# Writing the result in groups of four chunks, with the per-pixel factors spread by four 32-row matmuls

## Chip, core and metric

The kernel runs on one core of a Trainium2 chip. The metric is the device time of one execution in microseconds (us); lower is better. The engines are named as in the profile: PE is TensorE (matmuls and transposes; PEld is its loading of weights), DVE is VectorE, ACT is ScalarE, POOL is GpSimd, SP is SyncE, which only issues DMAs here.

## What is computed

The input `x` is 8 images of 128 x 128 pixels with 32 channels in fp32. Four layers are added to it one after the other, each on a group-normalised `x`. The change touches only the last layer and the writing of the result:

```python
x = x + _L0_conv_ref(_gn(x), ...)     # per-channel GELU mixer
x = x + _L1_conv_ref(_gn(x), kernel)  # 4 x 4 FIR filter
x = x + _L2_conv_ref(_gn(x), ...)     # windowed channel attention
x = x + _L3_conv_ref(_gn(x), W1, b1, gamma, beta)

def _L3_conv_ref(inputs, W1, b1, gamma, beta):
    kernel = centers @ W1 + b1                  # 9 weights for each inner pixel
    weighted = patches * kernel                 # the 3 x 3 patch around it
    yout = zeros.at[...].add(weighted)          # scattered back by addition
    yn = (yout - mean) * rsqrt(var + 1e-3) * gamma + beta   # mean, var over all pixels and images
    return where(yn >= 0, yn, 0.3 * yn)
```

Since each weight multiplies the pixel at which its product lands, `yout` at a pixel is the normalised input there times one number s, the sum of up to nine weights. So the last layer is v = (x - mean) * s, then statistics of v over everything, then a scale, a bias, the leaky step max(y, 0.3 y), and the sum with x.

## The kernel before, in words

`X` holds all pixels in SBUF: partition 32g + c is channel c of image g in a set of four images (a "sample", s = 0 or 1), and the free axis runs over the 16384 pixels of an image, column w by column w, 128 rows h each. Work goes by *chunks* of 512 columns of `X`; a sample has 32 chunks. Here a chunk n is made of the four image columns w = n, 32 + n, 64 + n, 96 + n (`columns(s, n)`).

Each sample passes stages 0 to 7, and every engine waits at each stage's end for the others (`stage_end`). Stages 0 to 4 load, transpose and run the first three layers, stage 5 computes the weights, stage 6 sums them to s and stores it transposed in `ST` (128 partitions for 32 chunks x 4 images, 512 columns). Two later places use s:

- **Stage 7** measures v. For each chunk `spread_s` (line 256) is one fp32 matmul that copies the four rows of `ST` of that chunk to all 128 partitions of a PSUM bank: the weights are a 128 x 128 0/1 matrix out of `sel`. Four banks are used in turn. For even chunks DVE makes v from PSUM (line 897); for odd ones ACT copies (lines 662, 663) and POOL multiplies (line 1038). DVE takes the statistics of all (`bn_stats`, line 889), in a loop of four chunks.
- **The output stage** comes once, after both samples and after the small steps for the overall statistics. For each chunk, in this order: `spread_s` (PE), `scaled` = v (DVE, line 939), `norm` (ACT, line 668), `leaky` (DVE, line 944), the sum with `X` (POOL, line 1054), four transposes to pixel-major order (PE, line 525), `lay` into the output buffer (ACT, line 677), and, for every four chunks, four DMAs of 256 KB (SP, line 304). `row`, a ring of eight 512-column buffers, holds a chunk from `scaled` to the transposes. Each engine does its steps in the order of its own program: DVE does `scaled(n + 2)` and then `leaky(n)`, ACT `norm(n + 4)` and then `lay(n)`, PE `out_s(n + 5)` and then `out_t(n)`. Engines wait for one another by counting semaphores alone (`s_fv`, `s_fy`, `s_fl`, `s_fo`, `s_ft`, `s_fe`). The stage does the first sample's 32 chunks and then the second's.

Of the kernel before, what the change touches and what calls it, by code (L numbers as in the profile page):

```python
# [22 lines left out]
P = 128  # L23
B, H, W, C = 8, 128, 128, 32
G = P // C
# [19 lines left out]
K9 = 9  # L45
# [4 lines left out]
ROWS = 8  # L50
# [16 lines left out]
def build(nc, x, consts, choose, out):  # L67
# [5 lines left out]
    with ctx:  # L73
# [40 lines left out]

        def rows4(v):
            return v.rearrange("p (b h) -> p b h", b=4)
# [33 lines left out]
        sel, _e = part(_e, [W // 4, P])  # L150
        vb, _v = part(_e, [DEEP, BANK])
        xd, _ = part(_v, [RING, BANK])
        U, _ = part(_v, [3, W, G])

        row, _o = part(0, [ROWS, BANK])
        assert _o <= (W + 2) * G * K9 and LOADS * G * LW * C <= (W + 2) * G * K9 + DEEP * BANK
        ob, _ = part(_e, [RING, G, 4, 4, C])
# [70 lines left out]
        s_fv = rsem("out_v_ready", "dve", DEEP)  # L228
        s_fy = sem("out_y_ready")
        s_fl = sem("out_l_ready")  # L230
        s_fo = sem("out_sum_ready")
        s_ft = rsem("out_transposed", "pe", ROWS)
        s_fe = rsem("out_chunk_ready", "act", DEEP)
        s_out = [sem(f"chunk_stored{u}") for u in range(RING)]
# [33 lines left out]
        def _(sp):  # L268
# [10 lines left out]
            for s in range(NS):  # L279
# [6 lines left out]
                for k in range(STAGES):  # L286
                    if k == 5:
                        sp.dma_start(sel[:, :, :], choose[:, :, :]).then_inc(s_sel, 16)
# [7 lines left out]
            with sp.Fori(0, NS) as s:  # L296
                with sp.Fori(0, 4) as i:
                    for u in range(RING):

                        sp.wait_ge(s_fe, after(s * NB + i * 8 + (4 * u + 3), DEEP))  # L300
                        for g in range(G):
                            o = out.rearrange("i h (b w) c -> h i b (w c)", b=4)
                            o = o[:, ds(s * G + g, 1), :, ds(i * (8 * C) + 4 * C * u, 4 * C)]
                            sp.dma_start(o.rearrange("h a b w -> h (a b) w"),
                                         ob[:, u, g, :, :, :].rearrange("p b w c -> p b (w c)")).then_inc(s_out[u], 16)
            for u in range(RING):
                sp.wait_ge(s_out[u], NS * 4 * 64 + 64)
# [3 lines left out]
        def _(pe):  # L311
# [4 lines left out]
            with pe.Fori(0, NS) as s:  # L316
# [185 lines left out]
                pe.wait_ge(s_sel, s * 16 + 16)  # L502
                for n in range(NB):
# [9 lines left out]
            with pe.Fori(0, NS) as s:  # L513
# [15 lines left out]
                for n in range(DEEP + 1):  # L529
                    out_s(n)  # L530
# [599 lines left out]
```

## Time and profile before

| | |
|---|---|
| median of 3 executions | 1149.85 us (1148.54 to 1150.21) |
| span of the profiled execution, first to last instruction | 1148.0 us |
| mean granted TensorE clock of that execution | 0.923 of full speed |
| stage 7 of the second sample | about 954 to 992 us of the span |
| output stage, first spreading matmul to last ACT copy | 997.1 to 1142.0 us |
| last copy to the end of the span (the last four DMAs) | 5.98 us |

The profiled execution's own time is not listed apart from the three above; what lies around its span is taken as the median less the span, 1.85 us. The profile page gives the busy time of each engine, the chain of waits that ended last, and groups of instructions; the trace behind it gives every instruction in order of time, with the idle time of its engine before it and the instruction that ended this idle time in square brackets. Matmul records of fp32 come in pairs (two passes for one matmul).

### The profile page before, as it was taken

The page shows a single profiled execution, that of the slowest core. Times are in us where ns is not written, and L with a number is a line of the kernel's source. Part 1 is how long each engine was busy: PE and PEld are TensorE (multiplying, and loading weights), DVE is VectorE, ACT ScalarE, POOL GpSimd, SP SyncE. Part 2 cuts the span into 40 slices and gives each one's busy share as a digit, 9 for nine tenths or more (in the row PEclk, how much of TensorE's full clock was granted, in tenths as well). Part 3 has the DMA queues.
Part 4 walks back from the last instruction along what each step waited for, and adds up shares of the span by engine and source line. Part 5 has one row for each costly group of instructions (what it writes and reads, how often), then busy time and mean ns, then how long its engine had stood idle before and what let it go on. Part 6 is the DMA issues. An engine that isn't in the chain of part 4 may idle for free. (4 is left out here: it accounts for less than half of the span.)

```text
span 1148.0 us, 22784 instructions
## 1 busy us (share of the span) xinstructions
PE 952.7 (83%) x6876; PEld 650.8 (57%) x6876; DVE 867.1 (76%) x1211; ACT 693.3 (60%) x860; POOL 317.6 (28%) x265
## 2 busy tenths in 40 slices
PE   5699977979989977845999949799999788676774
PEld 4333327968878875334433349688778683233332
DVE  7477788877757944876687878877769646799796
ACT  5799972323358853547999923234388563366564
POOL 0000009400026720510000066000077403466565
PEclk9799998989989988987999979989999898899897
DMA  9100000000000010233000000000000200024334
GB/s 294 37 0 0 0 0 1 0 1 1 0 1 1 0 73 5 69 114 107 0 0 0 0 1 1 1 1 0 1 1 0 74 0 1 0 86 135 106 114 146
DMA packets 51301, 39.32 MB, mean 34 GB/s; under 512 B 1600, under 2 KB 50880, under 8 KB 51008
## 3 DMA queue, kind: packets, MB, share of 16 engines
q1 hardware_dynamic: 51264, 38.85, 10.7%
q8 instruction: 20, 0.33, 0.1%
q14 instruction: 17, 0.14, 0.0%
HBM read 22.07 MB, written 16.78 MB: 34 GB/s over the span
## 5 line engine op out<-in xcount | busy, mean ns | idle before, releaser
L337 PE MATMUL ps<-work,cst 128*128 128x512 f32 x512 | 237.0, 610 | 17.5 <-ACT work L557 13.7
L337 PEld LDWEIGHTS ps<-work,cst 128*128 128x128 f32 x512 | 94.5, 193 | 158.8 <-issue 144.4
L256 PE MATMUL ps<-ST,work 128*128 x256 | 131.1, 635 | 9.7 <-DVE work L897 7.1
L557 ACT ACTIVATE work<-X,l0s 128x2048 f32 x64 | 136.6, 2140 | 2.6 <-SPq L294 2.6
L564 ACT ACTIVATE work<-ps 128x2048 f32<-128x2048 f32 x64 | 123.1, 1923 | 8.2 <-PE ps L337 8.0
L1019 POOL TENSOR_TENSOR work<-cst,ksum 128x512 f32<-128x512 f32 x64 | 66.2, 1055 | 203.2 <-SPq L294 174.4
L806 DVE TENSOR_TENSOR work<-ps,cst 64x512 f32<-64x512 f32 x128 | 88.2, 689 | 39.1 <-PE ps L404 37.3
L984 POOL TENSOR_TENSOR co<-mv,cst 128x1 f32<-128x1 f32 x8 | 1.5, 191 | 392.1 <-DVEq L246 302.4
L450 PE MATMUL ps<-work,cst 128*64 128x128 f32 x1024 | 103.6, 287 | 6.7 <-ACT work L621 6.7
L586 ACT ACTIVATE work<-ps 128x512 f32<-128x512 f32 x80 | 47.8, 598 | 100.5 <-PE ps L357 100.5
L450 PEld LDWEIGHTS ps<-work,cst 128*64 128x64 f32 x1024 | 88.4, 141 | 18.7 <-issue 9.9
L1054 POOL TENSOR_TENSOR work<-X,work 128x512 f32<-128x512 f32 x64 | 82.3, 1288 | 59.6 <-DVE work L944 59.6
L368 PE MATMUL ps<-cst,work 128*128 128x143 f32 x640 | 96.6, 295 | 2.6 <-DVE X L756 2.2
L726 DVE SCALAR_TENSOR_TENSOR work<-work,cst 128x2048 f32<-128x2048 f32 x32 | 75.2, 2351 | 24.3 <-ACT work L564 24.1
L944 DVE SCALAR_TENSOR_TENSOR work<-work 128x512 f32<-128x512 f32 x64 | 92.2, 1445 | 0.0
L595 ACT ACTIVATE work<-ps 128x512 f32<-128x512 f32 x64 | 38.2, 597 | 86.7 <-PE ps L404 86.7
L368 PEld LDWEIGHTS ps<-cst,work 128*128 128x128 f32 x640 | 85.8, 195 | 7.0 <-DVE X L756 5.9
L668 ACT ACTIVATE work<-work,bns 128x512 f32<-128x512 f32 x64 | 52.1, 814 | 59.9 <-DVE work L939 59.9
L621 ACT ACTIVATE work<-work 32x512 f32 (+1 forms) x128 | 80.4, 628 | 5.9 <-SPq L294 3.9
L525 PEld LDWEIGHTS ps<-cst,work 128*128 128x128 f32 x256 | 29.2, 150 | 87.1 <-POOL work L1054 87.1
L525 PE MATMUL ps<-cst,work 128*128 128x128 f32 x256 | 45.6, 305 | 39.1 <-POOL work L1054 38.9
L256 PEld LDWEIGHTS ps<-ST,work 128*128 128x128 f32 x256 | 46.6, 204 | 54.2 <-issue 30.5
(99 smaller groups left out, 1774.3 us busy)
## 6 DMA issues: line engine op xcount, KB each, us to landing
work<-x SPq DMA_DIRECT2D x32, 512.0 KB, 4.9
out<-work SPq DMA_DIRECT2D x64, 256.0 KB, 2.8
work<-choose SPq DMA_DIRECT2D x2, 2048.0 KB, 8.4
cst<-consts SPq DMA_DIRECT2D x1, 1009.5 KB, 9.6
cst<-consts SPq DMA_DIRECT2D x1, 64.0 KB, 2.0
```

What stands on the lines that cost most here:

```text
L256: return nc.tensor.matmul(ps[:, bank, :], sel[:, n, :], ST[:, ds(s * (4 * H), 4 * H)], start=True, stop=True)
L337: last = pe.matmul(ps[:, 4 * (m % 2) + b, :], wg[:, m, :], yb[:, m, b * BANK:(b + 1) * BANK], start=True, stop=True)
L368: last = pe.matmul(ps[:, DEEP + 2 * (q % 2) + par, at:at + OW * OH], patch[:, q, k, :], c("fir"), start=True, stop=True)
L450: last = pe.matmul(o[:, :, :, hd * CK:hd * CK + CK], wq[:, hd, :], mvg, start=(hd == 0), stop=(hd == HEADS - 1))
L525: last = pe.transpose(ps[:, DEEP + n % DEEP, w * P:w * P + P], row[:, n % ROWS, w * H:w * H + H], ident)
L557: act.activation(yb[:, m, :], X[:, ds(s * PIX + i * CHUNK, CHUNK)], ACT.Gelu, scale=l0s[:, m:m + 1], bias=l0s[:, MULTI + m:MULTI + m + 1]) ...
L564: act.activation(zb[:, m % 2, :], ps[:, 4 * (m % 2):4 * (m % 2) + 4, :].rearrange("p a b -> p (a b)"), ACT.Gelu).then_inc(s_zs, 1)
L621: last = act.activation(mh[C * g:C * g + C, u, :, g, :], src, ACT.Copy)
L726: dve.scalar_tensor_tensor(acc if m < MULTI - 1 else x_in, zb[:, m % 2, :], c("w2")[:, m:m + 1], acc if m else x_in, ALU.mult, ALU.add).th ...
L806: last = dve.tensor_tensor(o, k_in, bias, ALU.add)
L944: dve.scalar_tensor_tensor(row[:, u, :], row[:, u, :], LEAKY, row[:, u, :], ALU.mult, ALU.max).then_inc(s_fl, 1)
L1054: pool.tensor_tensor(rows4(row[:, u, :]), columns(s, n), rows4(row[:, u, :]), ALU.add).then_inc(s_fo, 1)
```

## The change

The output stage handles *groups* of four chunks (`TILES = 4`), 16 groups in all (`NS * GROUPS`), running through both samples without a break.

- `spread_group` replaces `spread_s`: four matmuls of 32 rows each. The rows of `ST` are stored in another order (four small copies in stage 6 instead of one), so that the rows of the four chunks of a group lie in four different 32-row parts; each matmul takes one part and writes one PSUM bank. `sel` shrinks from 32 matrices to 8 and is loaded by four DMAs.
- Stage 7 uses all eight banks, four to a group; DVE's loop covers eight chunks instead of four.
- In the output stage `scaled` is still done chunk by chunk (four in a row), `norm` and `leaky` are one operation of 2048 columns for a group, the sum is two of 1024 columns, the transposes and `lay` go in two halves. DVE does `scaled(q)` and then `leaky(q - 1)`; ACT `norm(q)` and then `lay(q - 3)`; PE the spreading of q and then the transposes of q - 3. `row` holds four groups, the output buffer three.
- PE's loop over samples is written out.

```diff
+TILES = 4
+GROUPS = W // 4 // TILES
+OUT_ROWS, OUT_RING = 4, 3
...
-        def spread_s(s, n, bank):
-
-            return nc.tensor.matmul(ps[:, bank, :], sel[:, n, :], ST[:, ds(s * (4 * H), 4 * H)], start=True, stop=True)
+        def spread_group(s, j, bank):
+
+            for r in range(TILES):
+                rows = slice(C * r, C * r + C)
+                last = nc.tensor.matmul(ps[:, bank + r, :], sel[rows, j, :], ST[rows, s * (4 * H):(s + 1) * (4 * H)],
+                                        start=True, stop=True)
+            return last
...
-                for n in range(NB):
-                    pe.wait_ge(s_so if n % 2 else s_v[0], slot(s * (NB // 2) + n // 2))
-                    spread_s(s, n, n % DEEP).then_inc(s_sc, 1)
+                for j in range(GROUPS):
+                    if j >= 2:
+                        pe.wait_ge(s_v[0], after(s * (NB // 2) + 2 * j - 3))
+                        pe.wait_ge(s_so, after(s * (NB // 2) + 2 * j - 3))
+                    spread_group(s, j, j % 2 * TILES).then_inc(s_sc, 1)
...
-                for n in range(DEEP + 1):
-                    out_s(n)
-                for n in range(NB):
-                    if n + DEEP + 1 < NB:
-                        out_s(n + DEEP + 1)
-                    out_t(n)
+            for q in range(NS * GROUPS):
+                if q:
+                    pe.wait_ge(s_fv, TILES * q)
+                spread_group(q // GROUPS, q % GROUPS, 0).then_inc(s_fc, 1)
+                if q >= 3:
+                    out_transposed(q - 3)
...
+            def norm(q):
+                act.wait_ge(s_fv, TILES * q + TILES)
+                s = q // GROUPS
+                y = row[:, q % OUT_ROWS, :, :].rearrange("p b n -> p (b n)")
+                act.activation(y, y, ACT.Identity, scale=bns[:, 12 + s:13 + s], bias=bns[:, 15:16]
+                               ).then_inc(s_fy, 1)
...
-                dve.tensor_copy(s_rows[:, :], ps[:, 7, :]).then_inc(s_ss, 1)
+                for r in range(TILES):
+                    by_tile = s_rows[:, :].rearrange("p (b r j g) -> p b r j g", b=4, r=TILES, g=G)[:, :, r, :, :]
+                    src = ps[:, 7, :].rearrange("p (b j r g) -> p b r j g", b=4, r=TILES, g=G)[:, :, r, :, :]
+                    last = dve.tensor_copy(by_tile, src)
+                last.then_inc(s_ss, 1)
...
+            def scaled(q):
+                s, j = divmod(q, GROUPS)
+                dve.wait_ge(s_fc, q + 1)
+                if q >= OUT_ROWS:
+                    dve.wait_ge(s_ft, 2 * (q - OUT_ROWS) + 2)
+                for r in range(TILES):
+                    dve.scalar_tensor_tensor(row[:, q % OUT_ROWS, :, r * H:r * H + H], columns(s, TILES * j + r),
+                                             vall[:, 4 * s + 3:4 * s + 4], rows4(ps[:, r, :]), ALU.add, ALU.mult
+                                             ).then_inc(s_fv, 1)
+
+            def leaky(q):
+                dve.wait_ge(s_fy, q + 1)
+                y = row[:, q % OUT_ROWS, :, :].rearrange("p b n -> p (b n)")
+                dve.scalar_tensor_tensor(y, y, LEAKY, y, ALU.mult, ALU.max).then_inc(s_fl, 1)
+
+            for q in range(NS * GROUPS):
+                scaled(q)
+                if q:
+                    leaky(q - 1)
+            leaky(NS * GROUPS - 1)
...
-                        pool.tensor_tensor(rows4(row[:, u, :]), columns(s, n), rows4(row[:, u, :]), ALU.add
-                                           ).then_inc(s_fo, 1)
+            for q in range(NS * GROUPS):
+                s, j = divmod(q, GROUPS)
+                pool.wait_ge(s_fl, q + 1)
+                for b in range(0, 4, 2):
+                    y = row[:, q % OUT_ROWS, b:b + 2, :]
+                    pool.tensor_tensor(y, group_columns(s, j, b), y, ALU.add).then_inc(s_fo, 1)
```

How the program of DVE reads in the middle of the output stage, with the semaphores each row waits for (line 939 is `scaled`, line 944 `leaky`), before:

```order
L939 ISA [waits out_transposed,out_s_spread]
L939 SCALAR_TENSOR_TENSOR work<-X,vall,ps 128x512
L944 SCALAR_TENSOR_TENSOR work<-work 128x512 [waits out_y_ready]
L937 REGISTER_ALU
L939 ISA [waits out_transposed,out_s_spread]
```

and in the changed kernel (line 954 is `scaled`, line 961 `leaky`):

```order
L954 SCALAR_TENSOR_TENSOR work<-X,vall,ps 128x4x128 [waits out_transposed,out_s_spread]
L954 SCALAR_TENSOR_TENSOR work<-X,vall,ps 128x4x128 x3
L961 SCALAR_TENSOR_TENSOR work<-work 128x2048 [waits out_y_ready]
L954 SCALAR_TENSOR_TENSOR work<-X,vall,ps 128x4x128 [waits out_transposed,out_s_spread]
L954 SCALAR_TENSOR_TENSOR work<-X,vall,ps 128x4x128 x3
```

One `leaky` of 2048 columns now stands behind four `scaled`, and the four share one wait for PE.

PE's program at the same place (line 256 is the spreading matmul, line 525 the transposes), before:

```order
L256 MATMUL ps<-ST,work 128x512 [waits out_v_ready]
L525 MATMUL ps<-cst,work 128x128 [waits out_chunk_ready,out_sum_ready]
L525 MATMUL ps<-cst,work 128x128 x3
L516 REGISTER_ALU
L256 MATMUL ps<-ST,work 128x512 [waits out_v_ready]
```

and in the changed kernel (line 265 is the spreading matmul, line 532 the transposes; `out_half_laid` is `s_fe`, `out_half_sum_ready` is `s_fo`):

```order
L265 MATMUL ps<-ST,work 128x512 [waits out_v_ready]
L265 MATMUL ps<-ST,work 128x512 x3
L532 MATMUL ps<-cst,work 128x128 [waits out_half_laid,out_half_sum_ready]
L532 MATMUL ps<-cst,work 128x128 x7
L532 MATMUL ps<-cst,work 128x128 [waits out_half_laid,out_half_sum_ready]
L532 MATMUL ps<-cst,work 128x128 x7
```

The spreading of a group is now four matmuls in a row, in front of 16 transposes that wait twice.

DVE's loop in stage 7, before (line 897 makes v of an even chunk, line 889 measures), one turn of four chunks from its second half to the branch and the first row of the next:

```order
L897 ISA [waits s_spread]
L897 SCALAR_TENSOR_TENSOR work<-X,co,ps 128x512
L889 ISA [waits odd_v_ready]
L889 BN_STATS stats<-work 128x6
L887 REGISTER_ALU
L889 ISA [waits even_v_ready]
L889 BN_STATS stats<-work 128x6
L889 ISA [waits odd_v_ready]
L889 BN_STATS stats<-work 128x6
L885 REGISTER_ALU
L885 COMPARE_AND_BRANCH
```

and in the changed kernel at the same point of the turn (lines 910 and 902), where the next group's first chunk now comes in between:

```order
L902 ISA [waits even_v_ready]
L902 BN_STATS stats<-work 128x6
L909 REGISTER_ALU
L910 ISA [waits s_spread]
L910 SCALAR_TENSOR_TENSOR work<-X,co,ps 128x512
L902 ISA [waits odd_v_ready]
L902 BN_STATS stats<-work 128x6
```

The measuring of a group's last chunk moved behind the making of v for the next group's first one, at every second group.

## Rows read from the trace of the kernel before

**Rows 1.** The page: busy time of each engine, share, count.

```profile
PE 952.7 (83%) x6876; PEld 650.8 (57%) x6876; DVE 867.1 (76%) x1211; ACT 693.3 (60%) x860; POOL 317.6 (28%) x265
```

**Rows 2.** Windows: from:to, length, busy PE, PEld, DVE, ACT, POOL, clock, DMA.

```profile
955.00:992.00 37.00, 29.93 (x64) 11.61 (x62) 31.02 (x48) 19.29 (x32) 20.36 (x16) 0.96 0.00 0
1004.00:1064.00 60.00, 42.27 (x170) 19.48 (x168) 60.00 (x59) 37.13 (x57) 36.78 (x30) 0.99 0.35 106
```

**Rows 3.** Timeline, one period of the output stage: start, duration, instruction, idle before.

```profile
1040.90 0.73 DVE L939 SCALAR_TENSOR_TENSOR work<-X,vall,ps 128x512 f32<-128x512 f32 x1
1041.23 1.27 POOL L1054 TENSOR_TENSOR work<-X,work 128x512 f32<-128x512 f32 x1 [0.80 <-DVE work L944]
1041.56 1.49 DVE L944 SCALAR_TENSOR_TENSOR work<-work 128x512 f32<-128x512 f32 x1
...
1043.30 1.27 POOL L1054 TENSOR_TENSOR work<-X,work 128x512 f32<-128x512 f32 x1 [0.80 <-DVE work L944]
```

**Rows 4.** Line L944 by itself: duration in ns, least, median, most.

```profile
L944 DVE SCALAR_TENSOR_TENSOR work<-work x64: 678/1484/1747, 1003.0 to 1136.1; 128x512 f32<-128x512 f32 x64
```

**Rows 5.** Groups of instructions by shape: busy us, mean ns, idle before.

```profile
L726 DVE SCALAR_TENSOR_TENSOR work<-work,cst 128x2048 f32<-128x2048 f32 x32 | 75.2, 2351 | 24.3 <-ACT work L564 24.1
L965 POOL TENSOR_TENSOR cst<-cst 128x128 f32<-128x128 f32 x1 | 0.5, 459 | 11.9 <-DMA cst<-consts 11.9
L557 ACT ACTIVATE work<-X,l0s 128x2048 f32 x64 | 136.6, 2140 | 2.6 <-SPq L294 2.6
L564 ACT ACTIVATE work<-ps 128x2048 f32<-128x2048 f32 x64 | 123.1, 1923 | 8.2 <-PE ps L337 8.0
L677 ACT ACTIVATE work<-ps 128x512 f32<-128x512 f32 x64 | 37.1, 580 | 8.2 <-PE ps L525 8.2
L883 DVE COPY ST<-ps 128x512 f32 x2 | 1.4, 692 | 2.2 <-PE ps L498 2.2
```

**Rows 6.** Timeline, TensorE in stage 3: matmuls on the whole array, then column-tiled ones.

```profile
791.15 1.06 PE L404 MATMUL ps<-cst,work 128*128 128x128 f32 x8
792.14 1.08 PE L414 MATMUL ps<-work 128*32 128x128 f32 x32
```

**Rows 7.** Timeline, the start of the output stage.

```profile
997.08 7.26 PE L256 MATMUL ps<-ST,work 128*128 x11
...
999.22 0.75 DVE L939 SCALAR_TENSOR_TENSOR work<-X,vall,ps 128x512 f32<-128x512 f32 x1
...
1000.88 0.75 DVE L939 SCALAR_TENSOR_TENSOR work<-X,vall,ps 128x512 f32<-128x512 f32 x1 [0.90 <-PE ps L256]
...
1003.99 1.27 POOL L1054 TENSOR_TENSOR work<-X,work 128x512 f32<-128x512 f32 x1 [5.68 <-DVE work L944]
```

**Rows 8.** Timeline, between the first sample's last chunk and the second's first.

```profile
1071.26 0.75 DVE L939 SCALAR_TENSOR_TENSOR work<-X,vall,ps 128x512 f32<-128x512 f32 x1 [5.26 <-PE ps L256]
```

**Rows 9.** Timeline, the end of the output stage.

```profile
1134.12 3.75 DVE L944 SCALAR_TENSOR_TENSOR work<-work 128x512 f32<-128x512 f32 x3
...
1135.85 4.37 POOL L1054 TENSOR_TENSOR work<-X,work 128x512 f32<-128x512 f32 x3 [0.80 <-DVE work L944]
...
1139.05 2.34 PE L525 MATMUL ps<-cst,work 128*128 128x128 f32 x8 [0.56 <-POOL work L1054]
...
1141.42 0.60 ACT L677 ACTIVATE work<-ps 128x512 f32<-128x512 f32 x1 [0.62 <-PE ps L525]
```

**Rows 10.** Timeline, stage 7 of the second sample.

```profile
956.25 0.75 DVE L897 SCALAR_TENSOR_TENSOR work<-X,co,ps 128x512 f32<-128x512 f32 x1 [2.79 <-PE ps L256]
...
958.01 0.72 ACT L662 ACTIVATE work<-X,co 128x512 f32 x1 [18.52 <-PE ps L256]
...
963.18 0.75 DVE L897 SCALAR_TENSOR_TENSOR work<-X,co,ps 128x512 f32<-128x512 f32 x1
...
963.99 3.70 PE L256 MATMUL ps<-ST,work 128*128 x8 [1.26 <-DVE work L897]
...
990.55 1.87 DVE L889 BATCH_NORM_STATS2 stats<-work 128x512 f32 x3
```

More of the change, by code:

```diff
@@ L149, in build @@
         s_rows, _e = part(_e, [W * G])
-        sel, _e = part(_e, [W // 4, P])
         vb, _v = part(_e, [DEEP, BANK])
-        xd, _ = part(_v, [RING, BANK])
+        xd, _e7 = part(_v, [RING, BANK])
         U, _ = part(_v, [3, W, G])
-        row, _o = part(0, [ROWS, BANK])
-        assert _o <= (W + 2) * G * K9 and LOADS * G * LW * C <= (W + 2) * G * K9 + DEEP * BANK
-        ob, _ = part(_e, [RING, G, 4, 4, C])
+        row, _o = part(0, [OUT_ROWS, 4, BANK])
+        ob, _o = part(_o, [OUT_RING, G, 4 * TILES, C])
+        sel, _s = part(MW + 7168 - 8 * P, [W // 4 // TILES, P])
+        assert max(_e7, _o) <= MW + 7168 - 8 * P
+        assert LOADS * G * LW * C <= (W + 2) * G * K9 + DEEP * BANK
         ring_sems = {}
@@ L295, in _ @@
                     sp.wait_ge(s_stage, s * (STAGES * ENG) + (k + 1) * ENG)
[L296 to L307, printed above, removed]
+            for q in range(NS * GROUPS):
+                s, j = divmod(q, GROUPS)
+                sp.wait_ge(s_fe, 2 * q + 2)
+                for g in range(G):
+                    o = out[s * G + g, :, :, :].rearrange("h (b w) c -> h b (w c)", b=4)
+                    sp.dma_start(o[:, :, TILES * C * j:TILES * C * (j + 1)],
+                                 ob[:, q % OUT_RING, g, :, :].rearrange("p (b w) c -> p b (w c)", b=4)
+                                 ).then_inc(s_out[q % OUT_RING], 16)
+            for u in range(OUT_RING):
+                sp.wait_ge(s_out[u], len(range(u, NS * GROUPS, OUT_RING)) * G * 16)
         @block.tensor
@@ L315, in _ @@
             pe.wait_ge(s_ident, 16)
-            with pe.Fori(0, NS) as s:
+            for s in range(NS):
                 with pe.Fori(0, W // LW // LOADS) as i:
@@ L654, in _ @@
                 stage_end(act, s, 6)
[L656 to L659 removed]
+                with act.Fori(0, GROUPS // 2) as i:
+                    for v in range(1, 2 * TILES, 2):
+                        u = v % TILES
+                        nn = s * (NB // 2) + i * TILES + v // 2
+                        act.wait_ge(s_sc, s * GROUPS + i * 2 + (v // TILES + 1))
@@ new lines, in norm, with lay @@
+            def norm(q):
[4 more added lines that the diff above has]
+                               ).then_inc(s_fy, 1)
+            def lay(q):
+                for hf in range(2):
+                    act.wait_ge(s_ft, 2 * q + hf + 1)
+                    if hf == 0 and q >= OUT_RING:
+                        act.wait_ge(s_out[q % OUT_RING], q // OUT_RING * G * 16)
+                    half = slice(2 * TILES * hf, 2 * TILES * hf + 2 * TILES)
+                    o = ob[:, q % OUT_RING, :, half, :].rearrange("p g m c -> p m g c")
+                    src = ps[:, TILES + 2 * hf:TILES + 2 * hf + 2, :].rearrange("p b (n g c) -> p (b n) g c", n=TILES, g=G)
+                    act.activation(o, src, ACT.Copy).then_inc(s_fe, 1)
@@ L693, in _ @@
+            for q in range(NS * GROUPS):
+                norm(q)
+                if q >= 3:
+                    lay(q - 3)
+            lay(NS * GROUPS - 3)
+            lay(NS * GROUPS - 2)
+            lay(NS * GROUPS - 1)
         @block.vector
```

133 lines of the change are left out of this document (44 added, 89 removed).

## The prediction

> **What bounds the kernel now.** The page's busy times [rows 1] name no one engine, and the stages have different limits, so I read the two touched stages by themselves. In the windows [rows 2] the reader should see that DVE is busy for all 60.00 us of the output stage's 60, while POOL shows 36.8, ACT 37.1 and PE 42.3, with TensorE's clock granted at 0.99 of full. But a busy DVE is not a working one. `leaky` takes 0.68 us at its quickest and 1.48 at its median [rows 4]. The timeline of one period [rows 3] shows why. POOL's sum starts at 1041.23 and ends at 1042.50. `leaky` starts at 1041.56, inside it, and ends at 1043.05, which is 0.55 behind POOL's end: DVE's two-input operation from SBUF has stood still until POOL was done. `scaled`, which has PSUM as an input, starts at 1040.90, is overlapped by POOL too, and still takes its 0.73. POOL's next sum starts 0.25 after `leaky`'s end (1043.30). So the period of 2.07 us is POOL 1.27, plus what remains of `leaky` 0.55, plus 0.25 for the semaphore: a closed loop of two engines that take turns at SBUF. It is 8.27 us for four chunks.
>
> Around the loop there are three fixed losses. At the start, PE's clock is at 1.2 GHz and the first spreading matmuls come 1.66 us apart (999.22 and 1000.88 [rows 7]). Between the samples DVE waits 5.26 us for PE [rows 8], because PE does the second sample's spreading only after the first's last transposes. At the end the pipeline runs out [rows 9] and the last ACT copy ends at 1142.02.
>
> In stage 7 [rows 10], DVE goes at 4.18 us for four chunks ((990.55 + 1.87 - 963.18) / 7 turns) and is busy 31.0 us of 37 [rows 2]: it is close to its own limit except at the start.
>
> **The output stage, by a ledger of SBUF turns.** What may not overlap is POOL's sums and DVE's `leaky`.
>
> - *POOL, 1024 columns.* 128 columns with the same kind of inputs take 0.46 [rows 5], 512 take 1.27 [rows 3], so 2.11 ns a column, and 1024 columns 1.27 + 1.08 = 2.35 us. Bounds: 2.16 if nothing is fixed in it (2.11 ns x 1024), 2.54 if all is proportional (2 x 1.27). 32 of them: 75.2 us (69 to 81).
> - *`leaky`, 2048 columns.* The same kind of operation takes 2.35 us alone [rows 5]; behind a POOL operation the 512-column one needed 0.55 instead of 0.68, so 2.22. 16 of them: 35.5 us (34 to 38).
> - *Hand-over.* Before, POOL idled 0.25 of every period. Now POOL has two operations for each `leaky`, and four `scaled` (0.66 apart by [rows 3], 2.71 together) lie between two `leaky`. `leaky(q)` arrives about 2.6 us after `leaky(q-1)` ended, just when POOL's first half ends (0.25 + 2.35). If DVE gets in between the halves, POOL never runs dry; if it has to wait for both, 0.25 comes back for each group, 4 us in all. In the tail, where POOL had three sums to do and DVE was waiting, the 3 `leaky` were finished within 3.75 us while the 3 sums took 4.37 [rows 9], so DVE did get in between. I take 1 us (0 to 4).
>
> Sum: 111.7 us (103 to 123), 7.0 a group against 8.27.
>
> *When it starts.* PE can start the first group at 997.1 as before [rows 7]. At the low clock one matmul is 1.66; how long do four with 32 rows take? No row shows row-tiled ones. Stage 3 has column-tiled ones: 8 records on the whole array take 1.06, 32 records on quarter arrays 1.08 [rows 6], so four run side by side. If rows do the same, a group takes about what one chunk took, say 2.5 us at the low clock and 1.3 at the full one (0.92 a matmul by 3.70 for four [rows 10], plus start-up). The bound from the other side is one after the other: 3.7 to 3.9, or 6.6 to 7.0 at the low clock. I take side by side, as the nearest row. Then `scaled(0)` is 999.6 to 1002.3, the second group's spreading waits for it (one set of four banks) until 1004.8, `scaled(1)` ends at 1007.5, and only then comes `leaky(0)`; `norm(0)` (2.14 [rows 5]) is hidden behind this. So the first turn begins at 1007.5. Before, POOL's first sum started at 1003.99: the larger groups cost some 6 us of filling.
>
> The Trainium skill (TensorEngine Tiling (Array Packing), Performance Considerations and Tiling Modes) says that tiles of 32 rows run up to 4 times faster, and TensorE: Matmul & The Clock Gate (Part 3) gives 3.07 times as measured. By that figure a group would take 4 x 0.92 / 3.07 = 1.2 us at the full clock and 2.2 at the low one, an estimate that leaves the sum where it is. The tiling page also says that a change of tiling mode drains TensorE. That speaks against a change that switches twice a group, but by the busy times below PE has some 3 us to spare in each group.
>
> *Who else could be late.* For a group: DVE 2.64 + 2.22 = 4.9; ACT `norm` 2.14 and two `lay` of 1.03 each (0.58 and the slope of [rows 5], (1923 - 580) / 1536 ns a column), 4.2; PE 1.3 + 4 x 0.65 = 3.9 at the full clock, 2.5 + 4 x 1.12 = 7.0 at the low one (8 transposes took 2.34 there [rows 9]). All are below or at 7.0. A group's spreading has from the end of `scaled(q-1)` to that of `leaky(q-2)`, about 4.3 us. So these are hidden; if the clock stays low, PE just about becomes a second limit. The break between samples is gone, since the groups run through.
>
> *The end.* The turns end at 1007.5 + 111.7 = 1119.2. Then the last half's 8 transposes at the low clock, 2.3, and `lay` 1.1: 1122.6. Before it was 1142.02 [rows 9]. **-19.4 us.** The last four DMAs are as before (1 MB after the last copy, 5.98 us). In the steady part 1 MB has to leave every 7.0 us instead of 8.3; DMA was busy 0.35 of the time [rows 2], so that stays hidden.
>
> **Stage 7.** At its start PE runs at the low clock, ACT's first odd chunk waits until 958.01 for the second matmul, and DVE's second group begins at 963.18 [rows 10]. With four banks filled at once, and the other four without any wait behind them, ACT can start with DVE at about 956.5, the second odd chunk follows directly, and the second group comes 2 to 3 us earlier. After that the steady turn gains little: DVE's six operations are 3.8 us of 4.18, and the loop now ends every eight chunks instead of four. I take -2.5 for each sample, **-5.0 us** (0 to -8). A group's spreading is asked for when the group two before is read, a whole turn ahead (4 us), and takes 1.3.
>
> **Stage 6.** Four copies of 128 columns replace one of 512, 692 ns [rows 5], so each needs at least a quarter of that, 0.17, and at most all of it. The slope of the two POOL sizes above leaves about a seventh of an operation as fixed; three more fixed parts of 0.1 make +0.3 a sample: **+0.6 us** for both (0 to 4). It is on the path, PE waits for it. The loads of `sel`, the written-out loop of PE: nothing, since they lie in stages where SP and PE's program are not what is waited for; in the output stage PE waited for data, not for its program.
>
> **Sum.** -19.4 - 5.0 + 0.6 = -23.8 us. Against the profiled execution (1148.0 and 1.85 around it, which is the median 1149.85): **1126 us**.
>
> **The rivals.**
>
> - *Less is saved in turns (0.14).* POOL's cost is proportional and hand-overs come back: 81.3 + 37.6 + 4 = 123 us, end at 1134 instead of 1122.6, and stage 7 gives 2: 1140 us. For it: I have only two sizes of POOL operation.
> - *The 32-row matmuls run one after the other at the full clock (0.08).* For it: no row shows them. In the output stage 3.9 fits in the 4.3 us window, but the first two groups are late by about 5; in stage 7 PE needs 3.9 of 4.18, starts cold with 7.0 for each of two groups, and costs about 7.5 a sample over the forecast: 1126 + 5 + 15 = 1146 us.
> - *They run one after the other and the clock is at the low level: slower (0.05).* Place: PE's own order, spreading of q and 16 transposes. Price: 7.0 + 4.5 = 11.5 us a group in the output stage against 8.6 before ((1142.0 - 1004.0) / 16), and 7.0 against 4.2 in stage 7: +46 +45, 1240 us. It decides from the point where PE's work for a group passes 8.6 us. Against it: where PE was busy 70 to 80% its clock was 0.96 to 0.99 [rows 2], and serial matmuls would keep it busier than that.
> - *Long operations do not exclude each other (0.07).* If only the short operations stood in each other's way, DVE's 4.9 us would be the period: 2.1 x 15 less, 1094 us. The Trainium skill (SBUF — State Buffer, Who interferes with whom) says that the pair of SBUF ports shared by DVE and POOL is an exclusive lock, held for the whole instruction by whichever starts first; by that rule the ledger holds for any length and this rival falls.
>
> The forecast has 0.66. **Range:** 1115 (turns at 2.16 and 2.1, stage 7 at -8) to 1140 (the first rival), which holds the forecast and that rival, 0.80. About 0.2% is what a measurement of this kernel can tell from no change. Faster by more: 0.66 + 0.14 + 0.08 + 0.07 = 0.95, less 0.02 for a chance that the late ones end at no change: 0.93; same 0.02; slower 0.05.
>
> **What would show it.** In the profile after: 2048-column `leaky` records of up to 4.6 us that end some 2.2 us after a POOL sum; POOL sums of 2.35; about 7.0 us from one group's first sum to the next; POOL busy nearly 70% of the output stage; the four spreading matmuls starting together; `leaky(0)` beginning at about 1002.5 us of the span (1007.5 less the 5 of stage 7); no wait of 5 us in the middle. Wrong if the spreading of a group takes over 4.3 us, if POOL's sums are over 2.5, or if DVE waits for `norm` or for PE in every group.

## The result, and the profile after

The changed kernel takes 1124.12 us (median of 4, 1124.04 to 1124.86) against 1150.03 us for the kernel before in the same series (median of 4): a ratio of 0.9775, with a 95% interval of 0.9761 to 0.9789, 25.9 us less. 1126 was forecast. The profiled execution took 1124.1 us with a span of 1122.0.

By place: the output stage's first spreading matmul starts at 993.38 instead of 997.08 us of the span, so everything ahead of it gave 3.7 us. From there to the last ACT copy it is 122.8 us instead of 144.9, which gave 22.1. The last DMAs gave 0.2. (Not all of the 3.7 us lies in stages 6 and 7; see "Why the prediction was right".)

The timeline of one group in the changed kernel (start, duration, engine, line, operation, what it waited for), which answers to [rows 3]:

```profile
1053.69 2.71 DVE L954 SCALAR_TENSOR_TENSOR work<-X,vall,ps 128x512 f32<-128x512 f32 x4
1053.85 4.65 POOL L1065 TENSOR_TENSOR work<-X,work 128x1024 f32<-128x1024 f32 x2 [2.23 <-DVE work L961]
1056.32 4.33 DVE L961 SCALAR_TENSOR_TENSOR work<-work 128x2048 f32<-128x2048 f32 x1
1056.43 2.09 ACT L680 ACTIVATE work<-work,bns 128x2048 f32<-128x2048 f32 x1 [2.99 <-DVE work L954]
1056.45 0.31 PEld L265 LDWEIGHTS ps<-ST,work 32*128 32x128 f32 x8 [2.04 <-DVE work L954]
1056.45 1.83 PE L265 MATMUL ps<-ST,work 32*128 32x512 f32 x8 [1.80 <-DVE work L954]
1058.43 1.92 ACT L691 ACTIVATE work<-ps 128x1024 f32<-128x1024 f32 x2
1059.55 3.27 PEld L532 LDWEIGHTS ps<-cst,work 128*128 128x128 f32 x16 [2.79 <-issue]
1059.58 3.65 PE L532 MATMUL ps<-cst,work 128*128 128x128 f32 x16 [1.29 <-ACT work L691]
1060.57 2.71 DVE L954 SCALAR_TENSOR_TENSOR work<-X,vall,ps 128x512 f32<-128x512 f32 x4
1060.73 4.67 POOL L1065 TENSOR_TENSOR work<-X,work 128x1024 f32<-128x1024 f32 x2 [2.23 <-DVE work L961]
```

The reader should see the same two engines taking turns. POOL sums from 1053.85 to 1058.50, both halves without a gap. `leaky` starts at 1056.32 inside them, ends at 1060.65, 2.15 us behind POOL's end, and POOL starts again 0.08 later. The period is 6.88 us for four chunks where it was 8.27. It matters which half `leaky` meets. A narrower window (1057 to 1060) shows POOL's second half by itself:

```profile
1056.15 2.35 POOL L1065 TENSOR_TENSOR work<-X,work 128x1024 f32<-128x1024 f32 x1
```

`leaky` came 0.17 us after it had started, so it waited for this half alone, 2.18 us, and then needed 2.15. It is the same in all 13 groups of the steady part: `leaky` starts 0.15 to 0.18 us behind the second half's start. The lines of the two operations by themselves (ns least, median, most) say that the durations are the rule too:

```profile
L961 DVE SCALAR_TENSOR_TENSOR work<-work x16: 2278/4338/4352, 1003.2 to 1102.0; 128x2048 f32<-128x2048 f32 x16
L1065 POOL TENSOR_TENSOR work<-X,work x32: 2341/2355/4327, 1005.5 to 1111.0; 128x1024 f32<-128x1024 f32 x32
```

The start and the end of the stage (timeline), which answer to [rows 7] and [rows 9]:

```profile
993.38 2.09 PE L265 MATMUL ps<-ST,work 32*128 32x512 f32 x8
995.61 2.72 DVE L954 SCALAR_TENSOR_TENSOR work<-X,vall,ps 128x512 f32<-128x512 f32 x4 [0.21 <-PE ps L265]
998.39 2.09 PE L265 MATMUL ps<-ST,work 32*128 32x512 f32 x8 [2.92 <-DVE work L954]
1003.18 2.29 DVE L961 SCALAR_TENSOR_TENSOR work<-work 128x2048 f32<-128x2048 f32 x1
1005.55 4.68 POOL L1065 TENSOR_TENSOR work<-X,work 128x1024 f32<-128x1024 f32 x2 [11.00 <-DVE work L961]
...
1102.13 11.24 POOL L1065 TENSOR_TENSOR work<-X,work 128x1024 f32<-128x1024 f32 x4 [2.23 <-DVE work L961]
1115.20 1.02 ACT L691 ACTIVATE work<-ps 128x1024 f32<-128x1024 f32 x1 [1.05 <-PE ps L532]
```

The first `leaky` begins at 1003.18, the last sum ends at 1113.37, the last copy at 1116.22. Windows of stage 7 and of the output stage (from:to, length, busy PE, PEld, DVE, ACT, POOL, clock, DMA), for [rows 2]:

```profile
955.00:992.00 37.00, 12.18 (x50) 3.52 (x50) 30.68 (x51) 17.50 (x30) 20.37 (x19) 0.54 0.00 0
1012.00:1100.00 88.00, 55.19 (x298) 37.76 (x296) 88.00 (x66) 49.19 (x38) 60.70 (x26) 0.75 0.48 143
```

TensorE's clock is lower in both: 0.54 against 0.96, and 0.75 against 0.99.

### The profile page after: what moved, and what is told of

It is laid out like the page before. It is cut to its first block and busy times, and to the rows that moved or that the text cites. A ratio compares the mean times of both kernels' runs of the same rounds, so it can differ in the third digit from the quotient of the medians.

```text
span 1122.0 us, 21703 instructions
## 1 busy us (share of the span) xinstructions
PE 888.2 (79%) x6876; PEld 634.5 (57%) x6876; DVE 842.4 (75%) x1169; ACT 672.3 (60%) x780; POOL 311.0 (28%) x233
## 3 DMA queue, kind: packets, MB, share of 16 engines
q1 hardware_dynamic: 51360, 35.71, 10.4%
## 5 line engine op out<-in xcount | busy, mean ns | idle before, releaser
L265 PE MATMUL ps<-ST,work 32*128 32x512 f32 x256 | 57.7, 991 | 47.8 <-DVE work L954 18.6
L378 PEld LDWEIGHTS ps<-cst,work 128*128 128x128 f32 x640 | 86.2, 196 | 7.2 <-DVE X L765 4.8
L1065 POOL TENSOR_TENSOR work<-X,work 128x1024 f32<-128x1024 f32 x32 | 76.6, 2417 | 42.2 <-DVE work L961 42.2
L496 PE MATMUL ps<-cst,work 128*128 128x96 f32 x512 | 63.2, 291 | 14.9 <-ACT work L660 14.9
L1049 POOL TENSOR_TENSOR work<-work 128x512 f32<-128x512 f32 x32 | 40.4, 1266 | 124.0 <-ACT work L674 124.0
L367 PE MATMUL ps<-cst,work 128*128 128x128 f32 x320 | 51.0, 284 | 28.8 <-DVE work L788 28.8
L336 PE MATMUL ps<-cst,work 128*128 128x128 f32 x256 | 41.0, 325 | 40.8 <-DVE work L720 28.1
L496 PEld LDWEIGHTS ps<-cst,work 128*128 128x128 f32 x512 | 62.9, 207 | 15.3 <-ACT work L660 15.3
```

The lines of the kernel that those rows point to most:

```text
L265: last = nc.tensor.matmul(ps[:, bank + r, :], sel[rows, j, :], ST[rows, s * (4 * H):(s + 1) * (4 * H)], start=True, stop=True)
L378: last = pe.matmul(ps[:, DEEP + 2 * (q % 2) + par, at:at + OW * OH], patch[:, q, k, :], c("fir"), start=True, stop=True)
L496: last = pe.matmul(ps[:, u, w * COLS:w * COLS + COLS], xc[:, u, w * H:w * H + H], c("w9"), start=True, stop=True)
L1065: pool.tensor_tensor(y, group_columns(s, j, b), y, ALU.add).then_inc(s_fo, 1)
```

## The experiments

Each was timed beside the kernel before on the same chip. The changed kernel was not timed again with them; where a run is compared with its 1124.1 us, that rests on the kernel before, which came out at 1149.9 to 1150.5 us in every series.

**1. Waits with constants (`old_written_out`).** The kernel before; in its output stage every loop is a Python loop:

```diff
-            with pool.Fori(0, NS) as s:
-                with pool.Fori(0, NB // ROWS) as i:
+            for s in range(NS):
+                for i in range(NB // ROWS):
```

(the same for PE, ACT, DVE and SP)

> The kernel before, with the loops of the output stage written out on all five engines, so that waits have constants instead of registers; the same instructions in the same order otherwise. Theory A: of the 0.25 us between the end of DVE's leaky step and POOL's next sum, 0.12 to 0.17 were the register instruction ahead of the sum; the period falls from 2.07 to about 1.92 us and the time by 7 to 11 us (1139 to 1143). Rival B: the 0.25 us are the semaphore's own way, and the changed kernel's 0.08 comes from something in its grouping: within 2 us of 1150.

1139.2 us, ratio 0.9901 (0.9886 to 0.9916). A period of its timeline:

```profile
1039.94 1.26 POOL L1054 TENSOR_TENSOR work<-X,work 128x512 f32<-128x512 f32 x1 [0.63 <-DVE work L944]
1040.44 1.31 DVE L944 SCALAR_TENSOR_TENSOR work<-work 128x512 f32<-128x512 f32 x1
1041.83 1.27 POOL L1054 TENSOR_TENSOR work<-X,work 128x512 f32<-128x512 f32 x1 [0.63 <-DVE work L944]
```

POOL starts 0.08 us after `leaky`'s end (1041.75) instead of 0.25, and the period is 1.89 instead of 2.07. In the kernel before, POOL's program has a register instruction in front of each sum (line 1054 by itself, ns least, median, most); in this run there is none:

```profile
L1054 POOLq FUSED_REGOPS  x64: 121/121/150, 1003.7 to 1137.9; - x64
```

So of what I had called "the semaphore", 0.17 us were this instruction, 0.12 by its record, and what lies around it. 64 times 0.17 makes 10.9, and 10.7 us were measured. That is about two fifths of the change's gain, and it needs no grouping.

**2. No break between the samples (`old_continuous`).** The same, with all 64 chunks as one sequence on every engine:

```diff
-                for n in range(NB):
-                    if n + DEEP + 1 < NB:
-                        out_s(n + DEEP + 1)
-                    out_t(n)
+            for n in range(NS * NB):
+                if n + DEEP + 1 < NS * NB:
+                    out_s(n + DEEP + 1)
+                out_t(n)
```

> The kernel before with the output stage written out (1139.2 us) and, beyond that, all 64 chunks in one sequence, so that PE spreads the second sample's first chunks while the first sample's last ones are still under way. Theory A: the break between the samples, in which DVE waits 5.3 us and POOL starts 12.2 us behind the last sum of the first sample's steady part, goes; 4 to 7 us less than 1139.2, so 1132 to 1135. What the changed kernel has beyond this (1124.1) is then stages 6 and 7 (3.8) and the grouping proper (4 to 7). Rival B: the break was mostly a tail that now comes once in another place: 1137 to 1139.

1134.4 us (1131.5 to 1135.4), ratio 0.9865 (0.9839 to 0.9891): 4.8 less than experiment 1, within what was expected, though this one's runs spread more. In its trace the one interval of four chunks that took 13.0 us across the break takes 7.6 like the others.

**3. Stages 6 and 7 alone (`only_stage7`).** The changed kernel up to the output stage, then the old output stage, with one 32-row matmul for a chunk:

```diff
+        def spread_one(s, n, bank):
+
+            rows = slice(C * (n % TILES), C * (n % TILES) + C)
+            return nc.tensor.matmul(ps[:, bank, :], sel[rows, n // TILES, :], ST[rows, s * (4 * H):(s + 1) * (4 * H)],
+                                    start=True, stop=True)
```

> The changed kernel's stages 0 to 7 (groups of four in stage 7, four small copies in stage 6, PE's sample loop written out) with the output stage of the kernel before, in its loops, each chunk spread by one 32-row matmul. Theory A (the trace of the changed kernel): stages 6 and 7 give 3.8 us up to the start of the output stage, and nothing else changes: 1145 to 1148. Rival B: the order of DVE in stage 7 costs what the start gains: within 1 us of 1150. Rival C: the small matmuls lower TensorE's clock in the output stage (they do half the array's work in a chunk): PE gets late in places and the time goes above 1150.

1187.7 us, ratio 1.0331 (1.031 to 1.0352): much slower, in the direction of rival C and far beyond what I had thought of. Its windows in the output stage:

```profile
1010.00:1060.00 50.00, 50.00 (x99) 19.90 (x99) 22.58 (x34) 21.54 (x34) 20.80 (x18) 0.50 0.28 84
```

PE is busy for all 50 us and its clock stays at 1.2 GHz in this stretch. So:

**4. The same with 128 rows in the output stage (`only_stage7_128`).**

```diff
-            rows = slice(C * (n % TILES), C * (n % TILES) + C)
-            return nc.tensor.matmul(ps[:, bank, :], sel[rows, n // TILES, :], ST[rows, s * (4 * H):(s + 1) * (4 * H)],
+            return nc.tensor.matmul(ps[:, bank, :], sel[:, n, :], ST[:, s * (4 * H):(s + 1) * (4 * H)],
                                     start=True, stop=True)
```

> The kernel of the run with only stages 6 and 7 changed (1187.7 us), but in the output stage each chunk is spread by one matmul with all 128 rows again; stage 7 keeps its groups of 32-row matmuls, and everything else is the same (sel is 32 matrices wide for it). Theory A (the rows of the array that a matmul uses decide the clock): the granted clock of the output stage goes from 0.5 back to 0.99, the spreading matmul's two records from 2.07 to 1.02 us, the period from 3.0 to 2.07, and the time to 1145 to 1148. Rival B: the low clock comes from stage 7 or from waits between PE and DVE that feed on themselves: the clock stays low and the time above 1180.

1146.0 us, ratio 0.9968 (0.9958 to 0.9977). The same stretch of it:

```profile
1010.00:1060.00 50.00, 35.43 (x142) 16.00 (x140) 50.00 (x50) 31.10 (x48) 30.73 (x25) 1.00 0.42 126
```

Clock 1.00, PE busy 35.4 us. The two kernels differ only in the rows of that matmul and the table behind it, and by 42 us. This run also measures what all the rest of the change gives without the grouping of the output stage: 3.9 us by the medians. That is not stages 6 and 7 alone: in its trace the output stage starts 2.6 us earlier than before, and the interval of four chunks across the break between the samples is 1.1 us shorter (12.9 instead of 14.0); there too PE's loop over samples is written out.

**5. One after the other (`serial`).** In the changed kernel, each 32-row matmul waits for the one before:

```diff
+        s_one = sem("one_spread")
+        spreads = [0]
...
+                if r < TILES - 1:
+                    last.then_inc(s_one, 1)
+                    spreads[0] += 1
+                    nc.tensor.wait_ge(s_one, spreads[0])
```

> The changed kernel, but each of the four 32-row matmuls of a group waits on a semaphore until the one before it has ended, in stage 7 and in the output stage. Theory A (my rival priced at 1146 us): one after the other they take 4 us at the full clock and 7 at the low one; stage 7 asks for a group each 4.3 us and gets slow, the output stage has some 4 us of room; 12 to 25 us more than the changed kernel, most of it in stage 7. Rival B: TensorE has room for them everywhere: less than 3 us more. Rival C: the clock stays at the low level and the output stage's period goes to 10 or 11 us: over 60 us more.

1229.7 us, ratio 1.0692 (1.0676 to 1.0708), 105.6 over the changed kernel. Two rows of its timeline, the spreading of one group and what waits for it:

```profile
1134.39 8.45 PE L268 MATMUL ps<-ST,work 32*128 32x512 f32 x8
1130.89 2.72 DVE L961 SCALAR_TENSOR_TENSOR work<-X,vall,ps 128x512 f32<-128x512 f32 x4 [4.22 <-PE ps L268]
```

A group takes 8.45 us at the low clock, against 1.14 at the full clock and 2.09 at the low one side by side. The clock was 0.58 in the output stage although PE was busy 164 us of 180 (1040 to 1220). Rival C is what happened, and both stages pay: stage 7 takes 59.0 us a sample instead of 38.0, the output stage 185.2 instead of 122.8.

**6. Four sums of 512 columns (`pool_quarters`).**

```diff
-                for b in range(0, 4, 2):
-                    y = row[:, q % OUT_ROWS, b:b + 2, :]
-                    pool.tensor_tensor(y, group_columns(s, j, b), y, ALU.add).then_inc(s_fo, 1)
+                for b in range(4):
+                    y = row[:, q % OUT_ROWS, b:b + 1, :]
+                    last = pool.tensor_tensor(y, group_columns(s, j, b), y, ALU.add)
+                    if b % 2:
+                        last.then_inc(s_fo, 1)
```

(`group_columns` gives one column block instead of two)

> The changed kernel with POOL's sum as four operations of 512 columns for a group instead of two of 1024. Theory A (ledger of turns at SBUF): four take 5.0 to 5.1 us instead of 4.66, the period goes from 6.89 to about 7.3 us and the time up by 5 to 7 us (1129 to 1131). Rival B: not the ledger but the chain of latencies sets the period: within 1 us of 1124. Rival C: with more gaps between POOL's operations DVE gets in earlier, POOL never idles, and the period stays or falls below 6.9: 1118 to 1124.

1126.9 us, 2.7 over the changed kernel (ratio to the kernel before 0.9806, 0.9791 to 0.9821, against 0.9775). Windows of its output stage:

```profile
1012.00:1100.00 88.00, 59.32 (x302) 37.35 (x300) 71.70 (x67) 50.66 (x39) 88.00 (x50) 0.73 0.48 143
```

POOL is busy for all 88 us, and from one group's first sum to the next it takes 6.96 us in the mean of the trace. One group's `leaky` and the POOL sum behind it (timeline, 1070 to 1071):

```profile
1068.77 2.54 DVE L961 SCALAR_TENSOR_TENSOR work<-work 128x2048 f32<-128x2048 f32 x1
1069.12 3.31 POOL L1065 TENSOR_TENSOR work<-X,work 128x512 f32<-128x512 f32 x1
```

`leaky` arrives during one sum, waits for that one only (0.4 us here), and goes ahead of the next, whose record stretches from 1.27 to 3.31 us meanwhile. In every group with `leaky` between sums the trace shows this. So the hand-over is hidden (rival C's mechanism), and the longer sums cost slightly more than that saves (A's): 6.96 against 6.90. The time lies between A's range and C's. The period accounts for 0.9 of the 2.7 us; in the trace another 0.9 lies ahead of the output stage, in code that is the same.

**7. One sum of 2048 columns (`pool_whole`).**

```diff
-                for b in range(0, 4, 2):
-                    y = row[:, q % OUT_ROWS, b:b + 2, :]
-                    pool.tensor_tensor(y, group_columns(s, j, b), y, ALU.add).then_inc(s_fo, 1)
+                y = row[:, q % OUT_ROWS, :, :]
+                pool.tensor_tensor(y, group_columns(s, j, 0), y, ALU.add).then_inc(s_fo, 2)
```

(`group_columns` gives all four column blocks)

> The changed kernel with POOL's sum as one operation of 2048 columns for a group instead of two of 1024. Theory A (ledger): 2048 columns take about 4.5 us, the period goes from 6.89 to 6.7 to 6.8, and the end comes 2 us later since all transposes of the last group wait for the whole sum: 1121 to 1125. Rival B: the transposes and ACT's copies, which all start later, now set the period with TensorE's clock low: 1128 or more.

1125.0 us, ratio 0.9781 (0.9764 to 0.9797): not told apart from the changed kernel. A sum takes 4.53 us and the period is 6.82 where nothing else is late, but the transposes start later: the last copy ends 4.8 us behind the last sum instead of 2.85.

**8. Without the leaky step (`no_leaky`).**

```diff
-                               ).then_inc(s_fy, 1)
+                               ).then_inc(s_fl, 1)
...
             for q in range(NS * GROUPS):
                 scaled(q)
-                if q:
-                    leaky(q - 1)
-            leaky(NS * GROUPS - 1)
```

(the first two lines are ACT's `norm`, which now releases POOL)

> The changed kernel without the leaky step (negative values are not scaled by 0.3; the output is not the reference's): DVE has only the four products of a group, POOL sums what ACT normalised. Theory A (POOL and DVE's leaky take turns at SBUF): the period falls from 6.89 to POOL's own 4.7 us and the time by 25 to 33 us (1091 to 1099), POOL's sums keep their 2.35 us and never wait. Rival B: PE at the low clock (2.1 and 3.7 us a group) is next and holds the period near 5.8: 1105 to 1110. Rival C: the leaky step was not what POOL waited for: 1118 or more.

1092.3 us in one execution. Windows:

```profile
1010.00:1070.00 60.00, 42.00 (x312) 27.94 (x312) 35.76 (x53) 49.65 (x38) 59.47 (x26) 0.96 0.65 193
```

POOL is busy 59.5 of 60 us and the groups follow every 4.64 us. Nothing else needed the remaining 2.2 us of the period: they were `leaky`'s turn.

**9. DVE's order in stage 7 (`s7_order`).** The changed kernel, with the last chunk of a group measured before the next group's first product:

```diff
                     for v in range(2 * TILES):
+                        if v % TILES == 0 and v:
+                            measure_v(v - 1)
                         if v % 2 == 0:
...
-                        if v:
+                        if v % TILES:
                             measure_v(v - 1)
```

> The changed kernel, but in stage 7 DVE measures a group's last chunk before it makes v of the next group's first one, as before the change (still eight chunks to a loop). Theory A: the changed order delays the measuring of chunk 3, through it ACT's copy for chunk 7 (two buffers for odd chunks) and POOL's product, so that DVE waits 0.55 us for POOL at each end of the loop; with the old order the steady turn of eight chunks falls from 8.64 us to 8.2 to 8.4, and the time by 1 to 3.5 us over both samples (1121 to 1123). Rival B: the buffers set the turn whatever the order: within 0.5 us of 1124. Rival C: the 0.24 us wait of the first measurement behind its own product comes back at every group: 1 to 2 us slower.

1121.7 us (1119.7 to 1122.4, 5 runs), ratio 0.9752 (0.9739 to 0.9765), 2.4 less than the changed kernel. First the changed kernel's timeline at the end of a turn, then this one's first products of two turns:

```profile
958.35 1.28 DVE L902 BATCH_NORM_STATS2 stats<-work 128x512 f32 x2
959.24 0.72 ACT L672 ACTIVATE work<-X,co 128x512 f32 x1 [0.64 <-DVE stats L902]
960.52 1.27 POOL L1049 TENSOR_TENSOR work<-work 128x512 f32<-128x512 f32 x1 [0.58 <-ACT work L674]
962.02 0.69 DVE L902 BATCH_NORM_STATS2 stats<-work 128x512 f32 x1 [0.55 <-POOL work L1049]
962.93 0.75 DVE L910 SCALAR_TENSOR_TENSOR work<-X,co,ps 128x512 f32<-128x512 f32 x1 [0.21 <-PE ps L265]
971.57 0.75 DVE L910 SCALAR_TENSOR_TENSOR work<-X,co,ps 128x512 f32<-128x512 f32 x1 [0.18 <-PE ps L265]
```

```profile
957.25 0.73 DVE L912 SCALAR_TENSOR_TENSOR work<-X,co,ps 128x512 f32<-128x512 f32 x1
965.30 0.73 DVE L912 SCALAR_TENSOR_TENSOR work<-X,co,ps 128x512 f32<-128x512 f32 x1
```

The first three rows are the chain: the measuring of chunk 3 (the first of two at 958.35) releases ACT for chunk 7, ACT releases POOL, and DVE's measuring of chunk 7 waits 0.55 us for POOL. Eight chunks take 8.64 us in the one and 8.05 in the other, less than the 8.2 to 8.4 expected and less than the 8.37 before the change. Over a whole stage 7 (first spreading matmul to the start of `bn_aggr`, line 713) that is 35.7 us instead of 38.0 in each sample, 4.4 together; the medians show 2.4. In the profiled execution the first sample's stage 7 began 1.2 us later than in the changed kernel's, behind code that is the same, so the two do not contradict each other.

**10. A quarter of the sum on PE, with experiment 9's order (`pe_quarter_s7`).** POOL sums three of the four column blocks; for the fourth PE adds X in PSUM:

```diff
-                        last = pe.transpose(ps[:, TILES + b, n * P:n * P + P],
-                                            row[:, q % OUT_ROWS, b, n * H:n * H + H], ident)
+                        o, y = ps[:, TILES + b, n * P:n * P + P], row[:, q % OUT_ROWS, b, n * H:n * H + H]
+                        if b < 3:
+                            last = pe.transpose(o, y, ident)
+                        else:
+                            at = (q // GROUPS) * PIX + (b * (W // 4) + TILES * (q % GROUPS) + n) * H
+                            pe.matmul(o, y, ident, start=True, stop=False)
+                            last = pe.matmul(o, X[:, at:at + H], ident, start=False, stop=True)
...
+                for b, n in ((0, 2), (2, 1)):
+                    y = row[:, q % OUT_ROWS, b:b + n, :]
+                    pool.tensor_tensor(y, group_columns(s, j, b, n), y, ALU.add).then_inc(s_fo, 1)
```

> The changed kernel with the old order of DVE in stage 7, and with a quarter of the sum with X taken from POOL: for the last of the four column blocks PE adds X's transpose to the chunk's in PSUM by matmuls with the identity, and POOL does 1024 and 512 columns. Theory A (ledger): POOL 2.35 + 1.27, leaky's rest 2.0, hand-over 0.2 give a period of 5.8 instead of 6.9, so 14 to 17 us less in the output stage, and 2.4 in stage 7: 1105 to 1109. Rival B: PE needs 9.3 us a group at the low clock and, if the clock doesn't rise with the work, sets the period: 1140 or more. Rival C: PE's waits make it the bound at 6.5: 1115 to 1120.

1104.2 us (1102.7 to 1104.8), ratio 0.9596 (0.9579 to 0.9614): the fastest whole kernel here, just below the 1105 to 1109 expected. Its timeline:

```profile
1048.70 3.60 POOL L1072 TENSOR_TENSOR work<-X,work 128x1024 f32<-128x1024 f32 x2 [2.23 <-DVE work L968]
1054.53 3.60 POOL L1072 TENSOR_TENSOR work<-X,work 128x1024 f32<-128x1024 f32 x2 [2.23 <-DVE work L968]
```

The period is 5.83, which is POOL's 3.60 and the 2.23 of `leaky` and hand-over, as the ledger says. PE has more to do, at a clock granted at 0.98 (1010 to 1090).

## Why the prediction was right, by its own steps

- **The bound (turns at SBUF): right, shown.** With more columns an operation (7), fewer (6), less of the sum (10) or no `leaky` (8), the period was each time the sum of POOL's time and `leaky`'s rest (without `leaky`, POOL's time alone): 6.82, 6.96, 5.83, 4.64. The exclusive-lock rule of the Trainium skill (SBUF — State Buffer, Who interferes with whom) is what all four agree with, also for 2048 columns; the rival that long operations do not exclude each other is out.
- **The sizes.** POOL's 1024 columns: 2.35 forecast, 2.355 measured. `leaky` behind POOL: 2.22 forecast, 2.15 measured. All turns together, from the first `leaky` to the last sum: 111.7 forecast, 110.2 measured.
- **"If DVE gets in between the halves, POOL never runs dry": did not happen, and the 1 us for hand-over came out by luck.** The rule that I took from the tail is right: a waiting `leaky` goes ahead of POOL's next sum (6 shows it with quarters). The arrival time was wrong. I set POOL's first half to end at 0.25 + 2.35 = 2.60 us behind the last `leaky`, and `leaky` to come at "about 2.6". The hand-over was 0.08, so the first half ended at 2.43, and `leaky`, at 2.55, found the second half already running, in every steady group. POOL then waits for each `leaky` after all. It costs little, since the 0.25 us in [rows 3] was 0.08 of hand-over and 0.17 around a register instruction that the written-out program doesn't have (1): 16 x 0.08 is 1.3 us, near the 1 us that I had taken for another reason.
- **Where the output stage's gain comes from: only half seen.** I set grouping and the break between the samples as the causes, put PE's written-out loop at nothing and did not price those of the other engines. Against the kernel before (1150), written-out waits are worth 10.7 us, the break between samples 4.8, what experiment 4 keeps of the change 3.9; to the changed kernel's 1124.1 there remain 6.4 us for the grouping proper. In the traces of experiment 2 and of the changed kernel the output stage is 5.7 us shorter: the turns from first to last sum give 12.3, the filling up to the first sum costs 5.6, the end 1.0. The split depends on the order in which the parts are taken. With grouping first, the register instruction would stand in front of 16 hand-overs instead of 64, so writing out would give some 16 x 0.17 = 2.7 us (an estimate from 1) and grouping the rest. That order was not run.
- **The start.** I priced side by side at 2.5 us for a group at the low clock and 1.3 at the full one; 2.09 and 1.14 were measured (the second in stage 7 of the changed kernel: `955.77 1.14 PE L265 MATMUL ps<-ST,work 32*128 32x512 f32 x8 [1.24 <-ACT work L674]`). At the full clock that is 3.2 times faster than four of 0.92 ([rows 10]), near the 3.07 of the Trainium skill (TensorE: Matmul & The Clock Gate, Part 3). The first turn began 9.8 us behind the first spreading matmul; 10.4 was forecast.
- **The end.** 2.85 us from the last sum to the last copy, 3.4 forecast.
- **Stage 7: forecast 5.0 us for both samples, 2.1 measured; the total of 4.4 ahead of the output stage looks right by luck.** Stage 7 of the second sample, first spreading matmul and first row behind the last measuring, before and after:

```profile
953.90 8.82 PE L256 MATMUL ps<-ST,work 128*128 x16 [1.29 <-SPq L294]
992.52 1.02 DVE L704 BATCH_NORM_AGGREGATE mv<-stats 128x2 f32<-128x192 f32 x1
```

```profile
950.84 3.69 PE L265 MATMUL ps<-ST,work 32*128 32x512 f32 x16 [1.02 <-SPq L306]
988.76 1.02 DVE L713 BATCH_NORM_AGGREGATE mv<-stats 128x2 f32<-128x192 f32 x1
```

38.6 us became 37.9; in the first sample it was 39.4 and 38.0. The second group began 6.9 us after the first spreading matmul instead of 9.3, which looks like the 2.4 us that I had priced. But part of it is order: the measuring of chunk 3 (0.69) now stands behind that point, and a wait of 0.55 us comes later in the same turn. At the first product of chunk 8, where the same work is done in both, 1.2 us are left. Then the steady turn lost: 8.64 us for eight chunks against 8.37. The measuring of chunk 3, moved behind the next product, frees ACT's buffer for chunk 7 later, and DVE then waits 0.55 us for POOL (9). I had this move in front of me and gave it no cost. Stage 6, forecast at +0.6, did not change (-0.1; its four copies take 0.88 us against 0.69). So stages 6 and 7 gave 2.2 us, and the other 1.5 of the 3.7 lie in stages 0 to 5, where the traces of the runs differ from one another by 1 to 2 us anyway (457.1 us from the first sample's `bn_aggr` to the second's spreading before, 455.9 after, 455.7 to 458.1 in the others).
- **The slower rival: its mechanism is real, my reason against it was false.** I held that serial matmuls would keep PE busy and so its clock high. In 5 and in 3 PE was busy 91% and 100%, and the clock was at 0.58 and 0.50. What saved the forecast was that the matmuls do run side by side. The rival's price, 1240 us, is close to the 1229.7 of experiment 5. My price for one after the other at the full clock, 1146 us, describes nothing that happened.

Left open: what the changed kernel would take if `leaky` came 0.2 us earlier in each group, ahead of POOL's second half (no steady group of any run with sums of 1024 columns shows that case); and, of experiments 3 and 5, what in the 32-row matmuls keeps the clock low.

## What to carry to other kernels

When two engines take turns at a resource, write the period as a ledger of their turns; then price what shortens a turn, what removes one, and what moves one to a third engine, which gave most here (20 us with the stage-7 order). Look at what stands in the program between a wait and the instruction it releases: a register instruction that costs 0.17 us in a closed loop is paid in every turn, and it looks like latency of the semaphore. Where two engines meet within 0.2 us, price both orders of arrival. Small-row matmuls pay only side by side; one at a time they cost the full time of a matmul (two records of 2.07 us at the low clock in 3, against 1.02 for 128 rows at the full one in 4) and may cost TensorE its clock.

## What the runs showed of the hardware

TensorE's granted clock stood at 0.50 in 50 us of an output stage in which PE was busy 50.00 of them with 32-row matmuls and transposes in turn, and stood at 1.00 where the same chunks were spread with 128 rows and PE was busy 35.4 of 50. With groups of four side by side and 16 transposes for every group it lay between, 0.75 at a period of 6.9 us, and rose to 0.96 and 0.98 where the period was 4.7 us or PE had X's matmuls in addition. A busy PE is thus no sign of a high clock. Where `leaky` waited for one POOL sum of 512 columns and another stood behind it (6), `leaky` went first every time, and the next sum's record then holds the time of its waiting (3.31 us for a sum of 1.27).
